# A two-layer block on one core: loads in another order, and a redrawn call list on every engine

## The reference

```
x = x + mamba2_like(bi_wkv(x, s, s, w, u, cond))      # in_proj 256 -> 1160, conv of 4 taps, 8 heads of 64, out_proj 512 -> 256
x = x + bitlinear_ffn(bi_wkv(x, s, s, w2, u2, cond))  # 256 -> 1024 -> 256

bi_wkv: ek = exp(min(k, 30)); a forward and a backward scan  a = a*decay + ek*v  and  b = b*decay + ek
        num = nf + nb - ek*v + euk*v;  den = df + db - ek + euk
        out = sigmoid(r) * num / max(den, 1e-8) * (0.8 + 0.2*tf)
attn:   xBC, z, dt = u @ in_proj_w; causal conv + silu; per head y = (C B^T * exp(cumulated log decay)) x, gated by silu(z),
        RMS norm, @ out_proj_w
ffn:    weights rounded to -1, 0, 1 by mean |w|; rows rounded to 8 bits; silu, gelu, layer norm, rounded again, @ w2
```

## Time and profile before

| what | value |
|---|---|
| median of 3 runs | 209.39 us (209.16 to 210.08) |
| profiled execution | 209.8 us, of which the span from first to last instruction 208.1 us |
| granted TensorE clock, mean | 0.958 |
| busy of the span | PE 153.8, DVE 170.5, ACT 167.0, POOL 125.2 us |
| loads | 8.69 MB read from HBM, nearly all in the first 26 us |

### The profile page before, as it was taken

How to read it: one execution, slowest core, us unless ns; L and a number is a source line. 1 busy time by engine, 2 the same in 40 slices (tenths; PEclk the granted TensorE clock), 3 DMA queues, 4 the chain that set the end, 5 groups by cost and what they waited for, 6 DMA issues and landing times.

```text
span 208.1 us, 2737 instructions
## 1 busy us (share of the span) xinstructions
PE 153.8 (74%) x724; PEld 105.3 (51%) x724; DVE 170.5 (82%) x291; ACT 167.0 (80%) x300; POOL 125.2 (60%) x172
## 2 busy tenths in 40 slices
PE   1000006959979979779999979998999999662884
PEld 0000006827458755358676538695566685321663
DVE  1879599999989999996999998649998166774991
ACT  3700768459998999775889999899899999999962
POOL 2763950309496359599650749834996539763770
PEclk9999999995799999988999999999999999998599
DMA  5899600000320000000000000000000000100012
GB/s 191 263 359 376 279 1 2 0 2 0 109 92 3 0 0 0 0 6 0 0 0 2 0 3 0 0 0 2 3 0 0 2 3 0 52 0 0 2 60 95
DMA packets 5439, 9.91 MB, mean 48 GB/s; under 512 B 816, under 2 KB 3504, under 8 KB 5168
## 3 DMA queue, kind: packets, MB, share of 16 engines
q1 hardware_dynamic: 5056, 9.71, 13.4%
q10 hardware_dynamic: 368, 0.03, 0.1%
HBM read 8.69 MB, written 1.05 MB: 47 GB/s over the span
## 4 chain that ended last, share of the span: by engine, by line
PE 23%; ACT 17%; issue 8%; POOL 5%; DVE 3%; POOLq 1%; ACTq 0%; DVEq 0%
PE banks L1534 19%; PE banks L1531 3%; ACT banks L805 2%; ACT banks L809 2%; ACT junk_v L815 2%; POOL wn L501 2%; ACT junk_q L823 1%; DVE banks L1292 1%; ACT yzT L774 1%; POOL qr L444 1%; ACT vv L739 1%; DVE wn L1304 1%; ACT L1016 1%; ACT L1013 1%; ACT L995 1%
## 5 line engine op out<-in xcount | busy, mean ns | idle before, releaser
L1534 PE MATMUL banks<-inw,uT 128*128 128x8 f32 (+1 forms) x64 | 21.7, 466 | 30.0 <-DVE uT L1157 30.0
L1534 PEld LDWEIGHTS banks<-inw,uT 128*128 128x128 f32 x64 | 11.2, 217 | 36.9 <-issue 36.5
L414 POOL TENSOR_TENSOR dec<-tri,la 128x1024 f32<-128x1024 f32 x8 | 17.4, 2174 | 17.8 <-ACT dec L622 8.7
L1110 DVE TENSOR_TENSOR_SCAN Fs<-D,E 128x514 f32<-128x514 f32 x16 | 21.2, 1337 | 2.1 <-POOL D L379 1.8
L1534 PE MATMUL banks<-uT,inw 128*128 128x256 f32 x80 | 22.9, 441 | 0.0
L1119 DVE TENSOR_TENSOR_SCAN Ys<-D,Fs 128x514 f32<-128x514 f32 x16 | 20.5, 1306 | 0.0
L1534 PEld LDWEIGHTS banks<-uT,inw 128*128 128x128 f32 x80 | 17.5, 225 | 3.9 <-issue 1.3
L1200 DVE SCALAR_TENSOR_TENSOR cv<-banks,cols,cv 128x255 f32<-128x255 f32 (+2 forms) x48 | 19.2, 472 | 0.1
L1534 PE MATMUL banks<-dec,late 128*128 128x512 f32 x32 | 15.4, 599 | 1.1 <-ACT zs L731 1.1
L1534 PEld LDWEIGHTS banks<-vv,dec 128*128 128x128 f32 x128 | 15.2, 192 | 1.9 <-issue 1.9
L1534 PE MATMUL banks<-outw,yzT 128*128 128x256 f32 x64 | 14.7, 381 | 1.3 <-ACT yzT L774 1.3
(11 more groups left out here) (174 smaller groups left out, 456.3 us busy)
## 6 DMA issues: line engine op xcount, KB each, us to landing
wn<-in_w_dram SPq DMA_DIRECT2D x2, 1024.0 KB, 9.1
inw<-in_in_w_dram SPq DMA_DIRECT2D x1, 1160.0 KB, 12.8
vT<-in_kT_dram SPq DMA_DIRECT2D x4, 256.0 KB, 5.5
xn<-in_x_dram SPq DMA_DIRECT2D x4, 256.0 KB, 10.1
xcT<-in_xT_dram SPq DMA_DIRECT2D x4, 256.0 KB, 7.7
out_dram<-ot SPq DMA_DIRECT2D x8, 128.0 KB, 1.7
b1b<-in_b_dram SPq DMA_DIRECT2D x1, 512.0 KB, 9.3
outw<-in_out_w_dram SPq DMA_DIRECT2D x1, 512.0 KB, 12.5
```

The costliest lines, as they stand in the source:

```text
L414: pool.tensor_tensor(dec[:, c], tri[:].unsqueeze(1).broadcast_to([P, NH, P]), la[:, b % 2, c, :].unsqueeze(2).broadcast_to([P, NH, P]), AL ...
L1110: dve.tensor_tensor_scan(Fs[:, w, k], D[:, w, 0:CT * TS], E[:, b % 2, k].rearrange("p c t -> p (c t)"), 0.0, ALU.mult, ALU.add).then_inc(f ...
L1534: return pe.matmul(dst, lhsT, rhs, start=start, stop=stop)
```

## The change

Three things change, and no helper's body does.

- SP issues its loads in another order. Before, xT(0), which `gate_x(0)` needs, was 14th of the 18 loads that the start makes; now it is 6th. w2 was third and is now last; outw was 9th and is 17th.
- The call list of PE, ACT, DVE and POOL is another order of the same calls. ACT still loads an activation table 23 times. PE's explicit waits are others.
- `HOME` gives other PSUM banks.

The diff, cut to a few places:

```
-    "conv_in": ((4, 2), (0, 1), (2, 6), (0, 6)),
+    "conv_in": ((5, 3), (6, 2), (5, 1), (6, 3)),
...
@@ gpsimd @@
             second_ratio(0)
-            pool.wait_ge(wabs_ok, 2)
+            own_times_v(1)
             log_decays(0, 0)
+            times_v(2)
             log_decays(0, 1)
-            times_v(2)
...
             ffn_round(7)
+            residual_bias(3)
...
@@ scalar @@
-            weight_done(0)
             features(2)
...
             square_y(1, 0)
-            conv_last_tap(2, 1)
...
             silu_z(1, 1)
+            weight_done(0)
             square_y(1, 1)
             turned_q1(0)
+            weight_done(1)
+            turned_y(1, 0)
             silu_z(2, 0)
-            turned_y(1, 0)
-            weight_done(1)
...
@@ vector @@
             make_ones()
-            wkv_min(0)
+            decay_factor()
+            make_decay()
             make_pads()
             out_factor()
-            decay_factor()
-            make_decay()
             make_gap()
...
             conv_taps(0, 0)
-            forward(2, 0, 0)
+            own_min(2)
             recip(1, 0, 2)
+            mask_scores(0)
+            weight_mean()
             ratio(1)
-            mask_scores(0)
             gated(1)
             y_scale(0)
-            own_min(2)
+            forward(2, 0, 0)
             attend(0, 0)
```

More of the change, by code:

```diff
@@ L28 @@
     "cond_sum": 0,
[L29 to L44, removed]
+    "weight_sums": 0,
+    "features": (1, 1, 3, 7),
+    "conv_in": ((5, 3), (6, 2), (5, 1), (6, 3)),
+    "conv_turns": ((3, 5), (3, 4), (2, 5), (7, 3)),
+    "gate_in": ((2, 4), (4, 7), (2, 4), (2, 1)),
+    "r2_turns": (6, 0, 2, 3),
+    "scores": (7, 5, 3, 0),
+    "log_decays": (((1, 3), (2, 5)), ((7, 1), (2, 6)), ((4, 0), (4, 2)), ((1, 7), (7, 6))),
+    "within": ((3, 4), (6, 4), (4, 2), (3, 1)),
+    "between": (4, 2, 5, 6),
+    "y_turns": ((7, 1), (3, 0), (3, 3), (0, 3)),
+    "project": (3, 1, 6, 2),
+    "q1_turns": (5, 5, 7, 2),
+    "ffn_up": (6, 0, 4, 4, 6, 4, 2, 6),
+    "ffn_turns": ((6, 2), (1, 0), (3, 0), (1, 4), (0, 2), (3, 1), (0, 2), (3, 5)),
+    "ffn_down": (2, 1, 5, 4, 6, 7, 1, 4),
 }
@@ L546, in _ @@
             skip_term(2, 0)
+            skip_term(2, 1)
             quantise_h(1)
-            second_ratio(3)
-            skip_term(2, 1)
+            residual_bias(1)
             add_skip(2)
             ffn_dev(0)
-            residual_bias(1)
+            second_ratio(3)
             norm_y(2, 0)
@@ L576, in _ @@
             norm_h(3)
-            residual_bias(3)
             quantise_h(3)
@@ L990, in _ @@
             square_y(3, 1)
+            ffn_turned(0, 1)
+            ffn_diag(5)
             turned_y(3, 0)
@@ L1354, in _ @@
             backward(0, 1, 0)
+            backward(0, 1, 1)
             recip(0, 0, 1)
-            backward(0, 1, 1)
             ratio(0)
+            gated(0)
             add_own(0, 1)
-            gated(0)
             forward(1, 0, 0)
@@ L1409, in _ @@
             gated(2)
+            mask_scores(1)
+            ffn_in_max(0)
             own_min(3)
-            ffn_in_max(0)
-            clip_weights(1)
-            mask_scores(1)
+            ffn_in_scale(0)
+            ffn_in_back(0)
             softplus_in(2)
             attend(1, 0)
+            attend(1, 1)
+            features(2)
+            clip_weights(1)
             y_scale(1)
-            ffn_in_scale(0)
-            attend(1, 1)
-            ffn_in_back(0)
-            features(2)
+            softplus_out(2)
             norm_gate(1, 0)
-            forward(3, 0, 0)
-            softplus_out(2)
-            forward(3, 0, 1)
             conv_taps(2, 1)
             norm_gate(1, 1)
+            forward(3, 0, 0)
+            forward(3, 0, 1)
             backward(3, 0, 0)
+            backward(3, 0, 1)
             forward(3, 1, 0)
-            backward(3, 0, 1)
             backward(3, 1, 0)
@@ L1513, in _ @@
             ffn_shift(7)
-            ffn_out(2)
-            ffn_out(3)
             ffn_max(6)
@@ L1518, in _ @@
             ffn_max(7)
+            ffn_out(2)
+            ffn_out(3)
             ffn_scale(7)
+            ffn_back(4)
+            ffn_out(4)
             ffn_back(5)
-            ffn_out(4)
+            ffn_out(5)
             ffn_back(6)
             ffn_back(7)
-            ffn_out(5)
             ffn_out(6)
@@ L1721, in _ @@
             pe.wait_ge(dex_ok, 7)
+            between(1)
             within(1, 0)
-            pe.wait_ge(dex_ok, 8)
+            pe.wait_ge(att_ok, 4)
             q1_turns(0)
             within(1, 1)
+            y_turns(1, 0)
             gate_in(2, 0)
-            y_turns(1, 0)
             ffn_up(0)
@@ L1754, in _ @@
             ffn_up(2)
+            pe.wait_ge(yzT_ok, 5)
             y_turns(2, 1)
```

364 lines of the change are left out of this document (180 added, 184 removed).

## The result

The changed kernel took 212.37 us at the median of 16 runs (210.46 to 215.14), the one before 209.52 beside it: a ratio of 1.011, interval 1.0074 to 1.0146. Run again later it took 211.42 against 209.78, ratio 1.0087 (1.0051 to 1.0122). The medians are of all executions and the ratios only of those outside a second, slower state, so the two need not agree. So the change makes the kernel 1.0% slower; forecast were 0.8% less. Its lines stand one lower in number than those of before. One part of the change is still to be named: SP's stores stood in the order of tiles 1, 0, 3, 2, 4 to 7 before, and now stand in that of 0 to 7.

The account below looks back on a forecast made before the run. DVE was taken as the bound from 33 to 90 us, PE from 90 to 174. Terms gave -0.3 at `conv_taps(0)`, -1.7 at 60 us, then 0: 209.8 to 208.1, by the median 207.7 us, range 204.2 to 210.6.

Parts of the forecast that it names:

- The end: After 174 us: `residual_bias(3)` last on POOL hidden by 0.8 us, `ffn_out(2)` and `(3)` later at no cost; 0 (-0.5 to +0.5).
- Start of the scans: First scans on DVE begin earlier, with `out_factor` moved behind and condT issued earlier: -0.7 us (bounds -1.2 and 0).
- `times_v(0)` and `own_times_v(0)`: POOL products beside the first DVE scans block them: +1.26 and +0.37, together +1.63 us (bounds 0 and +1.63).
- The seed's hole: DVE's 2.54 us wait for ACT's reciprocal seed goes; with the `recip` and backward scan blocks, -4.21 us (-4.21 to -2.5).
- outw landed at 22.2, not 24.0: outw near 24.0 us delays `scale_outw` and `times_v(1)` on POOL, blocking DVE: +0.6 us (bounds 0 and +2.5).
- `own_times_v(1)`: POOL product behind `second_ratio(0)`, where DVE has only scans, costs its full length: +2.35 us (bounds 0 and +2.35).
- `conv_taps(0)`: Sum of the head's terms on DVE up to this call: -0.3 us, begun within half a us of its old place.
- At 60 us: DVE's sum there -1.7 us: -0.3 at `conv_taps(0)`, -0.94 for holes, -0.4 for `ratio(1)` and `gated(1)` relief.
- 60 to 174: Third uT 1.7 us earlier, PE's 2.15 us wait for it stays, PE full after: 0 (bounds -1.2 and +1.5).
- the rivals: Head start passes whole, 205.2 us (chance 0.30); nothing moves, 209.1 (0.17); ends slower, 211.5 (0.17).
- The one on the slower side: ACT beside `within(1, 1)`: `weight_done(0)` and `(1)` delay PE's ring, PE loses 3.8 us, 211.5 us; chance 0.17.
- The one mark for what lies behind: If uT(2) is early but the end is not, a hole inside 90 to 174 us took it.

Follow-up runs that it names:

- dve_early: Two spare maxima on DVE ahead of `ratio(1)`, against the changed kernel with outputs in place and `own_times_v(2)` waiting for `forward(2, 0, 1)`: 210.53 us.
- act_late: Two spare copies on ACT at 149 us, against the changed kernel with outputs in place and `own_times_v(2)` waiting for `forward(2, 0, 1)`: 210.99 us.
- ut3_late: `gated(3)` behind `norm_gate(2, 1)` and two spare maxima, against the changed kernel with outputs in place and `own_times_v(2)` behind `forward(2, 0, 1)`: 208.23 us.

## Why the prediction was wrong

It failed at "The end": "ffn_out(2) and (3) move behind two maxima that wait for nothing else. 0 (bounds -0.5 and +0.5)". I asked what the two maxima wait for, and not who waits for the two outputs. They hold the two buffers of a ring; their stores' landing gates tiles 4 and 5, and these gate 6 and 7. The rows that showed the danger were in the trace of the kernel before: the outputs stood at 197.2, 4.2 us ahead of tile 4, and a store took 1.7 to land after an issue 0.9 later. A move by 2.7 us uses that distance up. Measured, the term is +2.3 (211.42 less 209.08) by the medians and +1.9 at the end of the two profiled executions, against 0. How much of it the distance alone makes is another matter. An estimate from the rows: with landings of 1.7 us, as before, tile 4 would have been put out at 203.3, the store of tile 5 would have landed at 206.4 and tile 7 been put out at 206.5, where PE's last product ended at 206.3. That is some 0.2 us late and not 1.9; the rest comes of the landings of 3.4 and 3.3 us, which no row of before could tell. The other half of that sentence, `residual_bias(3)` hidden, held.

By steps, with the second execution of the changed kernel:

- Start of the scans: 11.37 for 11.82, -0.45 (-0.7 forecast; -0.65 in the first execution).
- `times_v(0)` and `own_times_v(0)`: forecast +1.63. They blocked scans for 0.90 and 2.09 us where before had one block of 1.98, so +1.0.
- The seed's hole, the block of `recip` and that of the backward scan: gone, as forecast. But `recip` and `ratio`, now beside `scale_outw`, took 0.89, 0.85 and 0.85 us where 0.66 to 0.72 is usual; no term has these 0.5. uT(0) was written at 27.7 to 29.3 (28.1 as its end was forecast).
- outw landed at 22.2, not 24.0, so `times_v(1)` ran ahead of the scan that needs it. It blocked `gated(0)`, 1.57 us for 0.68: +0.9 for +0.6, which is most of uT(0)'s lateness.
- `own_times_v(1)`: forecast +2.35, measured 3.41 - 1.20 = 2.21, at the place named.
- `conv_taps(0)`: 47.33 for 47.54 in one execution, 47.13 in the other: -0.2 and -0.4 for -0.3. That this sum came out is in part luck, as the terms above miss by up to 0.6, some up and some down.
- At 60 us: -1.7 forecast. uT(1) was begun 1.1 us earlier and ended 0.9 earlier. `ratio(1)` took 0.75 for 1.41 and `gated(1)` 1.34 for 1.19, a relief of 0.5 for 0.4; most of the 0.94 for holes did not come.
- 60 to 174, "0": wrong in size. The -1.1 of DVE reached PE as -0.8 at uT(2), and PE's wait there shrank from 2.15 to 0.50 us and did not stay. uT(3) 1.6 us earlier meant nothing, since PE took it 4.7 us later anyway. Of time at 55 us on DVE about half passes (dve_early), of time at 149 us on ACT nearly all (act_late). 1.1 at a half is 0.6; without the ring the kernel was 0 to 0.7 below the one before. So this part is of the size seen, but whether it is a gain at all these runs can't tell from nothing.

Of the rivals, none happened. The one on the slower side had the sign and the size, 211.5, but the wrong place: `weight_done(0)` and `(1)` stood on ACT as it feared, and the second x2 came at 109.20, ahead of the 110.13 of before. That its figure is near the measured one is luck. The marks that the prediction named for itself came true up to uT(2) (the first scan took 2.10 us for 2.4, and PE's wait for the third uT was only 0.50). The one mark for what lies behind misled: uT(2) early and the end not was to mean a hole between 90 and 174 us, and the loss that all executions share lay behind 197. (In the profiled one, part of it was in between as well: the clock at 146 us.)

What remains open: what makes the longest executions, the tie at 62 us or something else; the 1.0 us of ut3_late; and whether it is the packet of instructions that makes a store's landing take 3.4 us for 1.7, and so most of this loss.

## What to carry to other kernels

When a list of calls is reordered, look at each ring of buffers and ask how far its writer now stands from the next writer, in time, against how long the reader (here a store's landing) takes, the longest and not the usual: here 1.7 us became 3.4 for two stores that had moved. A call that nobody behind it waits for by name may still be waited for by its buffer. Count a lead only at the engine that takes it next and at the rate at which it passes there: a result that lies ready for 4.7 us is no lead. Two instructions on DVE and POOL that began within 0.02 us of each other went in one order in one execution and in the other order in the next.
